# Gathering the mixture's rows and making the attention queries: one stage, batch by batch

## The reference, cut to what matters

```python
x = x + tanh(g_xattn[0]) * L0_xattn(layernorm(x), ctx, mask)
x = x + tanh(g_ffn[0])   * L0_ffn(layernorm(x), router_w, wg, wu, wd)   # ternary mixture, 8 experts, one per row
x = x + tanh(g_xattn[1]) * L1_xattn(layernorm(x), ctx, Wq, bq, Wk, bk, Wv, bv, Wo, bo)
x = x + tanh(g_ffn[1])   * L1_ffn(layernorm(x), w1, b1, w2, b2)
# in L1_xattn:  Q = query @ Wq.T + bq ; 16 heads of 32 ; softmax(Q K^T / sqrt(32)) V ; ctx @ Wo.T + bo
```

## Time and profile before

| | |
|---|---|
| median of 3 runs | 1852.11 us (1850.33 to 1853.24) |
| the profiled execution | 1848.32 us, its span 1846.6 us |
| PE, DVE, ACT, POOL busy | 79%, 68%, 52%, 23% of the span |
| mean granted TensorE clock | 0.898 of full speed |
| gather stage (first gather to last aggregate) | 710.0 to 737.6 us |
| query stage | 739.2 to 844.8 us |
| attention's first product | 848.4 us |

### The profile page before, as it was taken

How to read it: one execution, slowest core, us unless ns; L and a number is a source line. 1 busy time by engine, 2 the same in 40 slices (tenths; PEclk the granted TensorE clock), 3 DMA queues, 4 the chain that set the end, 5 groups by cost and what they waited for, 6 DMA issues and landing times. The chain is left out here.

```text
span 1846.6 us, 26704 instructions
## 1 busy us (share of the span) xinstructions
PE 1467.2 (79%) x8535; PEld 801.9 (43%) x8536; DVE 1261.1 (68%) x1528; ACT 952.5 (52%) x1426; POOL 431.3 (23%) x327
## 2 busy tenths in 40 slices
PE   4887896999741771577999998999926589999996
PEld 3444443555331330331444444444413266666664
DVE  3776756556492667536999998999728767655661
ACT  5666652344251561330676776777812286666551
POOL 0121210000023003300555555555762100000000
...
DMA packets 147474, 251.54 MB, mean 136 GB/s; under 512 B 11320, under 2 KB 61496, under 8 KB 146240
## 3 DMA queue, kind: packets, MB, share of 16 engines
...
...
## 5 line engine op out<-in xcount | busy, mean ns | idle before, releaser
L1604 ACT ACTIVATE t_e<-t_psE 128x512 f32<-128x512 f32 x512 | 304.4, 597 | 137.9 <-PE t_psE L1699 115.3
L1643 DVE TENSOR_REDUCE t_nmax<-t_psM 128x1 f32<-128x1024 f32 x256 | 301.6, 1212 | 19.3 <-PE t_psM L1680 19.2
L1562 POOL TENSOR_TENSOR t_low<-t_e 128x1024 bf16<-128x1024 f32 x128 | 250.0, 1955 | 201.4 <-ACT t_e L1604 188.0
L1710 PE MATMUL t_psO<-t_e,vst 128*96 128x512 bf16 x512 | 199.6, 390 | 2.5 <-POOL t_low L1562 2.5
L1699 PE MATMUL t_psE<-t_qst,kst 99*128 99x512 bf16 x512 | 195.1, 382 | 5.2 <-ACT t_e L1604 5.1
L1710 PE MATMUL t_psO<-t_low,vst 128*96 128x512 bf16 x512 | 193.1, 377 | 0.0
L1651 DVE TENSOR_TENSOR t_low<-t_e 128x1024 bf16<-128x1024 f32 x128 | 173.6, 1357 | 23.8 <-ACT t_e L1604 23.5
L1680 PE MATMUL t_psM<-kst,t_qst 96*128 96x512 bf16 x512 | 164.1, 404 | 31.4 <-DVE t_nmax L1643 22.7
L2193 PE MATMUL e_psG<-xeT,e_w1p 128*128 (+1 forms) x1536 | 173.2, 276 | 8.7 <-DVE e_w1p L2129 4.7
L2208 PE MATMUL e_psO<-e_w2p,e_hT 128*128 128x512 bf16 x768 | 167.1, 379 | 0.0
L2193 PEld LDWEIGHTS e_psG<-xeT,e_w1p 128*128 128x128 bf16 x1536 | 151.9, 99 | 30.3 <-issue 5.9
...
...
## 6 DMA issues: line engine op xcount, KB each, us to landing
...
wT<-ternary SPq DMA_DIRECT2D x8, 1536.0 KB, 23.5
...
```

Source lines behind the costliest of these rows:

```text
L1562: nc.gpsimd.tensor_tensor(low[:, slot(h, u), :, :], e32[:, slot(h, u), :, :], upper(h, u), ALU.subtract).then_inc(lo_pool, 1)
L1604: nc.scalar.activation(e32[:, slot(h, u), i, :], psE[:, i, :], ACT.Exp, scale=SC).then_inc(expd, 1)
L1643: nc.vector.tensor_reduce(nmax[:, h // G % 2, h % G, u:u + 1], banks_of(place_of_max(b, m)).rearrange("p a t -> p (a t)"), AX_X, ALU.max, ...
L1710: last = nc.tensor.matmul(psO[0:VW, h % 2, :], vst[:, g, 2 * u + i, h % G, :], part[:, i, :], start=(u == 0 and i == 0 and r == 0), stop=( ...
```

## The change

- **One stage.** `gather_phase` is gone; its work is done in `query_phase`, batch by batch. The semaphores are cleared before it, right behind the mixture. POOL issues 12 gathers, then rstd of batch 0, the other 4 gathers, and then for each batch its rstd (a `pow` of 4 columns) and a quarter of the `kst` rows. The gathered tiles lie in 12 slots.
- **DVE** splits the 8 weight tiles, then for each batch: normalises 4 tiles, splits 4, adds and measures the 4 tiles of the next batch, and evacuates the batch before. **ACT** makes all copies out of PSUM, the odd ones too. **PE** makes `gemm(b)` right behind the transposes of batch b.
- **Weights.** Wq and Wo are loaded by SP in the mixture stage, behind its first four row loads, into `qw32`, which is also the router's buffer for normalised tiles. The wait for the bias moves to the first evacuation.
- **Queries of batch 0** for attention are loaded by SP in the query stage, after the stores of batch 1. Attention's PE waits for four quarters of the `kst` rows.

```diff
+        xn = qw32[:, :, :, :].rearrange("p i u d -> p (i u) d")
...
@@ -1004,6 +1004,7 @@
                     sp.sem_inc(stored[i], 16)
                 for j in range(4):
                     load(j, j)
+                prefetch(sp)
                 with sp.Fori(0, (NS - 4) // 4) as i:
                     for k in range(4):
...
-def query_phase(nc, wq, bq, wo, queries_dram, ident, xres, moments, woT, kst, ones_set, prefetch):
+def load_queries(sp, b, g, queries_dram, qst, loaded):
...
+    for i, r in enumerate((0, 1, 0)):
+        sp.dma_start(qst[i * HD:(i + 1) * HD, g, :, :],
+                     q_v[bass.ds(b, 1), g, r].rearrange("o d h s -> d (o h) s")).then_inc(loaded[g], 16)
...
+def load_query_weights(sp, wq, wo, w32, w_loaded):
+
+    for i, w in enumerate((wq, wo)):
+        sp.dma_start(w32[:, i, :, :], w.rearrange("(u p) d -> p u d", p=P)).then_inc(w_loaded[i], 16)
...
+def query_phase(nc, place, gates, mixture_dram, w32, w_loaded, bq, queries_dram, ident, xres, woT, kst, ones_set,
+                prefetch, prefetch_queries):
+
...
+        NR = 3 * QD
+        rows = sb("q_rows", [P, NR, D], F32)
...
-                nc.gpsimd.memset(half[:, :], -0.5).then_inc(rstd_ready, 1)
-                nc.gpsimd.tensor_scalar(veps[:, :], moments[:, :, 1], EPS, None, ALU.add).then_inc(rstd_ready, 1)
-                pool.wait_ge(rstd_ready, 2)
-                nc.gpsimd.tensor_tensor(rstd[:, :], veps[:, :], half[:, :], ALU.pow).then_inc(rstd_ready, 1)
-                pool.wait_ge(rstd_ready, 3)
-                nc.gpsimd.memset(kst[3 * HD:, :, :, :], 1.0).then_inc(ones_set, 1)
+                def gather(t):
+                    if t >= NR:
+                        pool.wait_ge(updated, t - NR + 1)
+                    nc.gpsimd.indirect_dma_start(rows[:, t % NR, :], None, mixture_dram[:, :],
+                                                 bass.IndirectOffsetOnAxis(place[:, t:t + 1], 0)).then_inc(fetched[t], 16)
+
+                def deviations(b):
+                    q = slice(b * QD, (b + 1) * QD)
+                    pool.wait_ge(veps_ready, b + 1)
+                    nc.gpsimd.tensor_tensor(rstd[:, q], veps[:, q], half[:, :], ALU.pow).then_inc(rstd_ready, 1)
+
+                nc.gpsimd.memset(half[:, :], -0.5).then_inc(half_set, 1)
+                for t in range(NR):
+                    gather(t)
+                pool.wait_ge(half_set, 1)
+                deviations(0)
+                for t in range(NR, NT):
+                    gather(t)
+                for b in range(B):
+                    if b >= 1:
+                        deviations(b)
+                    pool.wait_ge(rstd_ready, b + 1)
+                    nc.gpsimd.memset(kst[3 * HD:, b, :, :], 1.0).then_inc(ones_set, 1)
+                    pool.wait_ge(ones_set, b + 1)
...
             def _(sp):
-                for i, w in enumerate((wq, wo)):
-                    sp.dma_start(w32[:, i, :, :], w.rearrange("(u p) d -> p u d", p=P)).then_inc(w_loaded[i], 16)
                 sp.dma_start(bias[:, :], bq.rearrange("(c p) -> p c", p=P),
                              allow_slow_non_contiguous=True).then_inc(bias_loaded, 16)
                 prefetch(sp)
...
+                    if b == 1:
+                        for k in range(KC):
+                            sp.wait_ge(stored[k], 16 * (b + 1))
+                        prefetch_queries(sp)
...
                 def copy(n):
                     act.wait_ge(xposed, n + 1)
-                    if n >= 4 * QD:
-                        act.wait_ge(gemm_done, ((n - 2 * QD) // QD - 1) * KC)
-                    nc.scalar.copy(target(n), psX[:, 0, :, :]).then_inc(even_copied, 1)
+                    if n >= NWT + 2 * QD:
+                        act.wait_ge(gemm_done, ((n - NWT) // QD - 1) * KC)
+                    nc.scalar.copy(target(n), psX[:, n % 2, :, :]).then_inc(copied, 1)
...
-                act.wait_ge(bias_loaded, 16)
-                for n in range(NTILE):
+                for n in range(NWT):
                     split(n)
-                    if n >= 2 and n % 2 == 0:
+                    if n >= 2:
                         copy(n - 2)
-                    if n >= 4 * QD - 1 and n % QD == 3:
-                        evacuate((n - 4 * QD + 1) // QD)
-                copy(NTILE - 2)
+                copy(NWT - 2)
+                copy(NWT - 1)
+                for b in range(B):
+                    for n in tiles_of(b):
+                        split(n)
+                    for n in tiles_of(b):
+                        copy(n)
+                    if b == 1:
+                        act.wait_ge(bias_loaded, 16)
+                    if b >= 1:
+                        evacuate(b - 1)
                 evacuate(B - 1)
...
-                def normalise(t):
-                    if t >= 4:
-                        dve.wait_ge(lo_done, t + 2 * QD - 3)
-                    nc.vector.tensor_scalar(xn[:, t % 4, :], xres[:, t, :], moments[:, t, 0:1], rstd[:, t:t + 1],
-                                            ALU.subtract, ALU.mult).then_inc(normed, 1)
-
-                def split(n):
+                def update(b):
+                    q = range(b * QD, (b + 1) * QD)
+                    for t in q:
+                        dve.wait_ge(fetched[t], 16)
+                        nc.vector.scalar_tensor_tensor(xres[:, t, :], rows[:, t % NR, :], gates[:, 2:3], xres[:, t, :],
+                                                       ALU.mult, ALU.add).then_inc(updated, 1)
+                        dve.wait_ge(updated, t + 1)
+                        nc.vector.bn_stats(stats[:, t, :], xres[:, t, :]).then_inc(stats_ready, 1)
+                    for t in q:
+                        dve.wait_ge(stats_ready, t + 1)
+                        nc.vector.bn_aggr(mom[:, t, :], stats[:, t, :]).then_inc(mom_ready, 1)
+                    dve.wait_ge(mom_ready, (b + 1) * QD)
+                    q = slice(b * QD, (b + 1) * QD)
+                    nc.vector.tensor_scalar(veps[:, q], mom[:, q, 1], EPS, None, ALU.add).then_inc(veps_ready, 1)
+
+                def normalise(b):
+                    dve.wait_ge(rstd_ready, b + 1)
+                    for t in range(b * QD, (b + 1) * QD):
+                        if t >= 4:
+                            dve.wait_ge(lo_done, t + NWT - 3)
+                        nc.vector.tensor_scalar(xn[:, t % 4, :], xres[:, t, :], mom[:, t, 0:1], rstd[:, t:t + 1],
+                                                ALU.subtract, ALU.mult).then_inc(normed, 1)
+
+                def low(n):
                     dve.wait_ge(hi_done, n + 1)
                     nc.vector.tensor_tensor(pair[:, n % 4, 1, :], source(n), pair[:, n % 4, 0, :],
                                             ALU.subtract).then_inc(lo_done, 1)
-
-                def copy(n):
-                    dve.wait_ge(xposed, n + 1)
-                    if n >= 4 * QD:
-                        dve.wait_ge(gemm_done, ((n - 2 * QD) // QD - 1) * KC)
-                    nc.vector.tensor_copy(target(n), psX[:, 1, :, :]).then_inc(odd_copied, 1)
                 def evacuate(b):
                     for k in range(KC):
@@ -1344,20 +1380,19 @@
                         nc.vector.scalar_tensor_tensor(qst[:, k, 1, :], psG[:, k, :], bias[:, k:k + 1],
                                                        qst[:, k, 0, :], ALU.add, ALU.subtract).then_inc(lo_out, 1)
-                dve.wait_ge(bias_loaded, 16)
-                for n in range(NTILE):
-                    split(n)
-                    if n == 2:
-                        dve.wait_ge(rstd_ready, 3)
-                    if n >= 2 and n + 2 < NTILE and n - 6 + 2 * QD < NTILE and n - 2 < 4:
-                        normalise(n - 2)
-                    if n >= 2 * QD and n - 4 < NT:
-                        normalise(n - 4)
-                    if n >= 2 and n % 2 == 1:
-                        copy(n - 2)
-                    if n >= 4 * QD - 1 and n % QD == 3:
-                        evacuate((n - 4 * QD + 1) // QD)
-                copy(NTILE - 1)
+                for n in range(NWT):
+                    low(n)
+                update(0)
+                for b in range(B):
+                    normalise(b)
+                    for n in tiles_of(b):
+                        low(n)
+                    if b + 1 < B:
+                        update(b + 1)
+                    if b == 1:
+                        dve.wait_ge(bias_loaded, 16)
+                    if b >= 1:
+                        evacuate(b - 1)
                 evacuate(B - 1)
...
-                for n in range(NTILE):
+                for n in range(NWT):
                     transposes(n)
-                    if n >= 4 * QD - 1 and n % QD == 3:
-                        gemm((n - 4 * QD + 1) // QD)
-                gemm(B - 1)
-
-
-def attention_phase(nc, queries_dram, keys_dram, values_dram, mixed_dram, ident, kst, vst, kv_loaded, ones_set):
+                for b in range(B):
```

(51 more changed lines are left out.)

120 lines of the change are left out of this document (49 added, 71 removed).

## The result

| | before | after |
|---|---|---|
| median of 4 runs | 1852.62 us (1850.33 to 1853.24) | 1823.89 us (1822.53 to 1824.53) |
| ratio to before | 1 | 0.9853, 95% interval 0.9837 to 0.9868 |
| span of the profiled run | 1846.6 | 1820.8 |
| attention's first product | 848.39 | 810.12 |
| from there to the issue of the last store of `mixed` | 504.9 (to 1353.3) | 517.8 (to 1327.9) |

The kernel is 28.7 us faster (the medians). The forecast was 1815 us, a gain of 37. The stage that was changed gained what was forecast: attention starts 38.3 us earlier. Attention itself then takes 12.9 us longer, although the code of its loops was not changed but for the name of the query tile (at its head, SP's 12 query loads are gone and PE waits for four `kst` quarters instead of one `kst` memset). Behind it nothing differs (493 us to the end of the span in both).

What follows compares the result with a forecast made beforehand. Before 776 us no engine was taken as near full, idle waiting being the cost; step by step attention's first product moved from 848.39 to 811.4, gaining 37.0, forecast 1815 us, own range 1808 to 1823, 8 in 10 range 1806 to 1829.

Steps and rivals of the forecast that it cites:

- start of the stage: Merged gather and query stage: semaphore clearing now ahead of the gathers adds 0.7 us, so the stage starts at 710.7.
- weights done on DVE: Head of the stage: weights already in SBUF, ACT starts at 710.7, DVE has its last weight tile done at 722.1.
- first gemm: Query stage: gemm(0) starts at 738.7 against 776.33 before, 37.6 us earlier.
- rivals 2 and 3: POOL's gather chain delays the `pow`, 1817 to 1823, chance 0.08; weight loads hold up the mixture, 1818 to 1820, chance 0.03.
- the three gaps: Between gemms: transposes, four ACT copies, an evacuation on ACT and DVE and pickups make 6.3 us each.
- the thin cover of DVE's work: Under gemm(0): batch 1's first half ready at about 749, gemm ending at 751.3, about 2 us to spare.
- DVE's work for batch 1: Under gemm(0): additions, `pow` wait, normalising behind a quarter memset, splits and batch 0's rest, 15.7 us in all.
- the 1 us for gathers holding up the normalisations: Batch 0: POOL's last four gathers beside DVE's four normalisations cost 1 us, at most 4.3.
- The rule of the Trainium skill: DVE and POOL share a port pair as a lock; by it batch 0's normalisations beside gathers make the sum 3 us later.
- The 0.8 us for the DMA contention: Gather stage: first gathers share DMA engines with 6 MB of keys and values; 0.8 us taken as the loss.
- 1 wrong: Rival 1, gather stage: gathers come last behind the keys and values, loss 16.4 us, time 1831, chance 0.08.
- 4 wrong: Rival 4: gaps keep PE at the lower clock in all gemms, 1852, or 1856 if attention suffers too; chance 0.02.

Runs made afterwards that it cites:

- after_pad12: The changed kernel with 12 idle semaphore instructions more on ACT ahead of its attention loop; 1808.8 us, ratio 0.9771 to the kernel before.

## Why the prediction was right in the stage and 9 us off in the whole

Right, by its own steps (forecast, then trace): start of the stage 710.7, 711.05 (POOL's first instruction); weights done on DVE 722.1, 722.8; batch 0 added and measured 727.8, 728.4; `pow` done 729.5, 730.0; normalised 732.7, 732.2; first gemm 738.7, 738.32; last gemm done 806.2, 805.8; attention 811.4, 810.12. The gain there was forecast as 37.0 and is 38.3.

Luck has a part in the whole. The time, 1823.9, lies just outside the forecast's own range (1808 to 1823). It lies inside the wider one (1806 to 1829) because that made room for rivals 2 and 3, neither of which came true; no term and no rival stood for what did happen.

Sizes that were off and cancelled: gemm(0) took 10.3 us where 12.6 was forecast (in after_pad12, 12.25); the four gemms together took 47.2 instead of 48.6, the three gaps 20.3 instead of 18.9. The first gap was 8.0 and not 6.3: with gemm(0) that short, the thin cover of DVE's work was gone, and PE waited 4.83 us for an evacuation that stood behind update(2). In after_pad12, with the longer gemm(0), that gap is 5.9 and the wait 2.73. The other two gaps were 6.1. DVE's work for batch 1 was forecast as 15.7 us, though its parts add up to 15.2; it took 14.9 (734.50 to 749.41). Of the 1 us for gathers holding up the normalisations 0.2 was needed (2.10 us for four, against 1.91 in batch 3 with nothing beside them). The rule of the Trainium skill that I weighed there ("SBUF — State Buffer", section "SBUF: two separate sides") would by my reckoning have cost 3 us more. It did not come true for gathers, though only one and the start of a second lay beside the normalisations; beside memsets it did (5.18 us). The 0.8 us for the DMA contention was not needed either.

The rivals: no addition waited for a gather (1 wrong); the twelfth gather was issued by 727.5, the `pow` waited for DVE's epsilon at 728.8 (2 wrong, by 1.3 us); the mixture's last tile was scaled at 706.56 against 706.04 (3 wrong; the mixture had also started 0.5 us later); the clock was granted at 0.88 from 739 on (4 wrong).

The step that failed is the last sentence of the part on the bound: "Behind it attention's code and order are the same, so what is won there stays won." The code of the loop was the same, its place in ACT's instruction stream was not. 14 instructions more ahead of the loop moved two stalls from 2.0 and 2.3 us to 6.1 and 6.4, 8.4 us. The remaining 4.5 of the 12.9 us come with the restart: PE had stood for 5.3 us, its granted clock falls from 1.00 to 0.50 (1.2 GHz) in the window of 976 to 978, and its products take 0.63 us instead of 0.38 for some 6 us, and for some 4 us at the second back edge:

```profile
976.00:978.00 2.00, 1.58 (x4) 0.79 (x5) 1.12 (x1) 1.44 (x3) 0.00 (x0) 0.50 0.97 237
```

In these stretches products start 0.43 us apart instead of 0.22, so an estimate of the loss is half of 10 us, 5 us, near the 4.5. In after_pad12 the granted clock stays at 1.00 behind both back edges (966 to 972 and 1086 to 1092). That the clock is all of the 4.5 is argued, not shown; what is shown is that both go together when the loop is moved (attention 501.4 us, stalls 4.5). The sign of it was there before. The waits of the kernel before (us in total, times, longest) have this row on the exponentials, from which PE, DVE and POOL take every tile:

```profile
ACT t_e L1604 <- issue: 4.6, 2, 2.3
```

The two stalls in it are those of the second back edge; at the first, the trace puts the waits down to PE. I did not ask what that wait was, nor what the change does to it, because ACT as a whole is busy only half the time.
